# A graph network on one core: the state tables of layers 1 to 3 transposed in 32x32 blocks by VectorE and joined by four stores, with a feature's two parts side by side

## The chip, the cores and the metric

The kernel runs on one core of a Trainium2 chip. The metric is device time in microseconds (us), the median of several runs. A core has five engines, each with its own program, joined by semaphores: TensorE (PE, matmuls; its weight loads are PEld), VectorE (DVE), ScalarE (ACT), GpSimd (POOL) and SyncE (SP). Here SyncE issues nearly all plain DMAs, and GpSimd the gathers.

## What is computed

A graph network over 12500 nodes and 200000 edges (sorted by dst): a layernorm, an encoder, five rounds of message passing with a GRU update, a decoder. All of it is float32.

```python
h = relu(layernorm(x)); h = relu(h @ enc_w1.T + enc_b1) @ enc_w2.T + enc_b2
for w in conv_w:                                   # 5 layers
    agg = segment_sum((h @ w)[src], dst, n_nodes)
    gi = agg @ gru_wih.T + gru_bih
    gh = h @ gru_whh.T + gru_bhh
    r, z = sigmoid(gi_r + gh_r), sigmoid(gi_z + gh_z)
    n = tanh(gi_n + r * gh_n)
    h = (1 - z) * n + z * h
out = x + sigmoid(relu(relu(h) @ dec_w1.T + dec_b1) @ dec_w2.T + dec_b2)
```

## The kernel before

**States and tables.** The matrices of a layer are folded into the GRU's (W_FOLD), so that sums of old states are enough. States are held twice in DRAM: transposed (features on partitions) in `states`, one block of 128x512 for each of 25 chunks of 512 nodes (the last has 256), and with a node to a row in `table[0]` and `table[1]`, of which a layer reads one and writes the other. A row has 1 KB: 128 features, each as two float32 parts. The high part is the state rounded to fp32r, the form in which TensorE takes it, and the low part is what is left. Before, the 128 high parts stand first and the 128 low parts behind them.

**Two ways to a sum.** A chunk's sums come in one of two ways.
- *Strips*, for the first 14 chunks (11 in layer 0): TensorE multiplies the whole table, resident in SBUF as `parts` (98 blocks of 128 nodes), by a matrix of edge counts. Counts are loaded as bytes (SP, L705), three pieces of 448 KB in a ring, widened by ScalarE (L1126) and used in `sum_unit` (L1908): for each of 98 blocks two matmuls, one with the high and one with the low parts as weights, both with 512 count columns.
- *Gathers*, for the rest: GpSimd gathers 128 rows of the table at a time (L940), eight gathers to a group of edges, with room for four groups in `messages`. TensorE multiplies a group by a selection that VectorE makes (L1410, L1801), VectorE adds the high and the low half (`combine`, L1441), TensorE transposes (L1808) and VectorE adds it to `running` (L1459).

**Order of the work.** `Stage` cuts a layer into steps, one for each group (84 in layers 1 to 4). Every engine's program walks the same steps. `spread_gru` sets the step at which each chunk's GRU begins, at least three apart, and `gru_steps` then gives the chunk's stage t in each step: t = 1 gates (TensorE L1817 to L1824, ScalarE L1051), t = 2 the candidate's input, t = 3 VectorE's `after_candidate` (L1513, L1516, L1526), which ends in h_new, t = 4 the table, t = 5 its store. Strip pieces are spread over the steps, and the first of the next layer fill the end.

**The table, t = 4.** TensorE's `make_table` waits for h_new and transposes its four 128x128 blocks into PSUM (L1743); ScalarE copies them rounded into the high parts of `table_stage` (L1076); VectorE subtracts these from PSUM into the low parts (`low_halves`, L1322). At t = 5 SyncE stores a chunk at once (L626). The last chunk of a layer is chunk 24; its gates follow chunk 23's table in each program.

**Layer's end.** GpSimd's first gather of a layer waits for all 25 chunks' stores (L950). SyncE loads `parts` in seven portions (L711).

## Time and profile before

| | us |
|---|---|
| median of 3 runs | 4876.18 |
| lowest, highest | 4873.26, 4878.4 |
| the profiled execution | 4887.71 |
| its span | 4886.0 |

| engine | busy us | share of the span |
|---|---|---|
| TensorE | 4569.3 | 94% |
| its weight loads | 3509.0 | 72% |
| ScalarE | 3776.9 | 77% |
| GpSimd | 3514.1 | 72% |
| VectorE | 2125.1 | 43% |

Busy time leaves out the work of issuing and waiting. A gather's own time counts as GpSimd's, and what it moves as the DMA engines'. Times of the trace count from the start of the span. Gathers of the five layers run at 155 to 1278, 1313 to 2172, 2195 to 3054, 3076 to 3934 and 3957 to 4855 us. L12 is line 12 of the kernel before.

### The profile page before, as it was taken

Reading aid. Unit: us, or ns where it says so; the run is one execution under the profiler, and the core shown is the slowest. Engines: PE = TensorE matmul, PEld = TensorE weight load, DVE = VectorE, ACT = ScalarE, POOL = GpSimd, SP = SyncE. Lnnn points to the kernel's source line nnn. Section 1 sums busy time; section 2 is a strip of 40 time slices with the busy share of each in tenths; the row PEclk is TensorE's granted clock in tenths of the full one; section 3 lists DMA queues with packets and bytes.
Section 4 is the critical chain, followed back from the end, with each engine's and each line's share of the span. In section 5 each row is a group of like instructions: output and inputs, shape, how many; then the busy total and the mean of one; then the engine's idle time right before and its main releaser. Section 6 shows DMA issues by size and latency. Waiting matters only on the chain.

```text
span 4886.0 us, 65093 instructions
## 1 busy us (share of the span) xinstructions
PE 4569.3 (94%) x21620; PEld 3509.0 (72%) x21620; DVE 2125.1 (43%) x5051; ACT 3776.9 (77%) x3018; POOL 3514.1 (72%) x3618
## 2 busy tenths in 40 slices
PE   5579999998899999989999999899999989999998
PEld 3357767676677777767777777677777767777775
DVE  7678888787323333332333233233323323232324
ACT  5468889888688787858888786788888767787784
POOL 3577777777577777767777777677777767777675
PEclk8789999999999999999999999999999999999999
DMA  6899999999877777787777779777777877777774
GB/s 208 280 288 281 292 288 286 286 288 307 275 231 242 237 242 237 241 287 246 237 241 240 236 242 309 227 239 236 248 229 251 289 238 226 219 216 219 218 219 150
DMA packets 712057, 1217.93 MB, mean 249 GB/s; under 512 B 283649, under 2 KB 442370, under 8 KB 711618
## 3 DMA queue, kind: packets, MB, share of 16 engines
q1 hardware_dynamic: 538976, 741.62, 49.2%
q0 software_dynamic: 172336, 470.52, 30.7%
q8 instruction: 176, 2.88, 0.2%
q10 hardware_dynamic: 434, 1.81, 0.1%
q14 instruction: 135, 1.11, 0.1%
HBM read 1017.20 MB, written 196.41 MB: 248 GB/s over the span
## 4 chain that ended last, share of the span: by engine, by line
PE 71%; ACT 7%; POOL 6%; DMA 6%; issue 5%; DVE 4%; SPq 0%; DVEq 0%; ACTq 0%; POOLq 0%
PE strip_ps L1908 34%; PE four_ps L1908 16%; POOL messages L940 6%; ACT counts L1126 4%; PE agg_ps L1801 4%; DMA raw<-adjacency 3%; PE four_ps L1801 3%; ACT room L1101 2%; PE r_ps L1817 2%; PE z_ps L1817 2%; PE r_ps L1823 2%; PE z_ps L1823 2%; PE four_ps L1824 1%; PE r_ps L1830 1%; PE four_ps L1894 1%
## 5 line engine op out<-in xcount | busy, mean ns | idle before, releaser
L940 POOL DMA_INDIRECT messages<-table,src_stage x3567 | 3467.0, 972 | 1278.6 <-issue 1121.6
L1126 ACT ACTIVATE counts<-raw 128x2048 fp32r<-128x2048 uint8 x1354 | 2227.5, 1692 | 429.0 <-PE strip_ps L1908 239.9
L1908 PE MATMUL strip_ps<-counts,parts 128*128 128x512 f32 x9016 | 2283.0, 406 | 62.3 <-ACT counts L1126 49.5
L1908 PEld LDWEIGHTS strip_ps<-counts,parts 128*128 128x128 f32 x9016 | 1690.2, 190 | 508.5 <-issue 117.5
L1908 PE MATMUL four_ps<-counts,parts 128*128 128x512 f32 x4116 | 985.4, 396 | 0.0
L1126 ACT ACTIVATE counts<-third_raw 128x2048 fp32r<-128x2048 uint8 (+1 forms) x522 | 855.9, 1688 | 158.2 <-PE strip_ps L1908 87.9
L1908 PEld LDWEIGHTS four_ps<-counts,parts 128*128 128x128 f32 x4116 | 768.7, 188 | 184.0 <-issue 28.8
L1410 DVE TENSOR_TENSOR selection<-agg_ps,dst_stage 128x1024 fp32r<-128x1024 bf16 x277 | 337.3, 1218 | 947.4 <-PE agg_ps L1808 946.6
L1410 DVE TENSOR_TENSOR selection<-four_ps,dst_stage 128x1024 fp32r<-128x1024 bf16 (+1 forms) x172 | 207.8, 1208 | 860.2 <-PE four_ps L1808 860.0
L1101 ACT ACTIVATE room<-four_ps 128x784 uint16<-128x784 f32 x448 | 359.5, 822 | 89.9 <-PE four_ps L1894 47.1
L1801 PE MATMUL agg_ps<-messages,selection 128*128 128x256 f32 x2211 | 339.9, 297 | 40.2 <-DMA messages<-table,src_stage 39.1
L1801 PEld LDWEIGHTS agg_ps<-messages,selection 128*128 128x128 f32 x2211 | 291.7, 195 | 64.1 <-DMA messages<-table,src_stage 43.6
L1801 PE MATMUL four_ps<-messages,selection 128*128 128x256 f32 x1356 | 205.2, 294 | 19.9 <-DMA messages<-table,src_stage 19.9
L1801 PEld LDWEIGHTS four_ps<-messages,selection 128*128 128x128 f32 x1356 | 173.7, 190 | 38.1 <-DMA messages<-table,src_stage 22.9
L1070 ACT ACTIVATE gate_n<-gate_r,b 128x512 f32<-128x512 f32 (+1 forms) x125 | 88.5, 708 | 104.4 <-DVE gate_r L1493 96.8
L1441 DVE TENSOR_REDUCE rows<-agg_ps 128x128 f32<-128x256 f32 x277 | 116.0, 419 | 117.0 <-PE agg_ps L1801 116.7
L1051 ACT ACTIVATE gate_r<-r_ps,b_rz 128x512 f32<-128x512 f32 (+1 forms) x100 | 67.4, 674 | 101.7 <-PE r_ps L1823 101.7
L1322 DVE TENSOR_TENSOR table_stage<-four_ps,table_stage 128x512 fp32r<-128x512 f32 (+1 forms) x75 | 51.1, 681 | 202.9 <-ACT table_stage L1076 202.4
L1441 DVE TENSOR_REDUCE rows<-four_ps 128x128 f32<-128x256 f32 x172 | 69.5, 404 | 141.5 <-PE four_ps L1801 141.5
L1817 PE MATMUL r_ps<-h_old,w 128*128 128x512 f32 (+1 forms) x200 | 105.3, 609 | 6.0 <-DMA h_old<-states 5.9
L1817 PE MATMUL z_ps<-h_old,w 128*128 128x512 f32 (+1 forms) x200 | 104.9, 608 | 0.0
L1824 PE MATMUL four_ps<-h_old,w 128*128 128x512 f32 (+1 forms) x200 | 100.7, 585 | 0.0
(226 smaller groups left out, 3575.3 us busy)
## 6 DMA issues: line engine op xcount, KB each, us to landing
raw<-adjacency SPq DMA_DIRECT2D x677, 448.0 KB, 5.2
third_raw<-adjacency SPq DMA_DIRECT2D x261, 448.0 KB
adjacency<-room SPq DMA_DIRECT2D x112, 784.0 KB
parts<-table SPq DMA_DIRECT2D x35, 1792.0 KB, 14.2
messages<-table,src_stage POOLq DMA_INDIRECT x3567
table<-table_stage SPq DMA_DIRECT2D x108, 512.0 KB, 3.0
h_old<-states SPq DMA_DIRECT2D x120, 256.0 KB
states<-h_new SPq DMA_DIRECT2D x108, 256.0 KB, 3.2
```

What stands on the lines that cost most here:

```text
L940: nc.gpsimd.indirect_dma_start(messages[:, slot, t, :, :].rearrange("p i f -> p (i f)").bitcast(F32), None, table[k.layer % 2], bass.Indir ...
L1051: nc.scalar.activation(gate_r[:, 0:n], r_ps[:, 0:n], ACT.Sigmoid, bias=b_rz[:, R:R + 1]).then_inc(gates_rz, 1)
L1070: nc.scalar.activation(gate_n[:, 0:n], pre_n[:, 0:n], ACT.Tanh, bias=b[:, B_IH + N:B_IH + N + 1]).then_inc(cand, 1)
L1101: nc.scalar.activation(eighth_counts[:, eighth % 2, :, j * SET_NODES // 2:(j + 1) * SET_NODES // 2].rearrange("p k (t d) -> p k t d", t=SE ...
L1126: nc.scalar.activation(to, raw_piece[:, :, a * EIGHTH:e * EIGHTH].rearrange("p q (k d) -> p k q d", d=EIGHTH), ACT.Copy).then_inc(expanded, 1)
L1410: ops.tensor_tensor(selection[:, s % 2, 0:n, :], on_each(cols_ps[k.agg_bank(s)].bitcast(BF16), n), along(dst_stage[:, at:at + n], ROWS), A ...
L1441: ops.tensor_reduce(rows[:, :], agg_ps[k.agg_bank(s)][:, 0:2 * H].rearrange("p (i f) -> p f i", i=2), AX_X, ALU.add).then_inc(combined, 1)
L1801: last = mm(agg_ps[k.agg_bank(s)][:, 0:2 * H], selection[:, s % 2, t, :], messages[:, slot, t, :, :].rearrange("p i f -> p (i f)"), start= ...
L1817: mm(bank[:, 0:n], wblock(W_HH + gate), h[:, 0:n], start=True, stop=False)
L1823: mm(bank[:, 0:n], wblock(W_FOLD + gate), a[:, 0:n], start=False, stop=True).then_inc(gates_ps, 1)
L1824: mm(hn_ps[:, 0:n], wblock(W_HH + N), h[:, 0:n], start=True, stop=True).then_inc(gates_ps, 1)
L1908: last = mm(strip_banks[k.bank_of(i)], parts[:, block, half, :], counts[:, 0 if k.first else p % 2, at, :], start=(p == 0 and at == 0 and ...
```

## The change

In layers 1 to 3 TensorE no longer makes the table. After h_new VectorE transposes it in 32x32 blocks (`turn_state`) into `turned`, which is the buffer of `diff`. Partition 32q + r then holds, in columns 32m to 32m + 31, the features 32q to 32q + 31 of node 32m + r. ScalarE copies `turned` rounded into the high parts, VectorE subtracts in place of `low_halves`, and SyncE puts a chunk's rows together with four stores, one for each block of 32 partitions, in runs of 64 words (256 B). So that a run holds both parts, the table's rows now have a feature's high and low part side by side, everywhere: `parts`, the first table, layer 0, and the addition in `combine`. Stores are counted by `tables_stored(n)`. Layer 0 still transposes on TensorE, the last layer makes no table. The path `general` (other graphs) isn't run.

```diff
+def tables_stored(n):
+    return 16 * (n + (QUARTERS - 1) * max(0, n - 2 * CHUNKS))
...
-        by_half = table_stage[:, :].bitcast(F32R).rearrange("p (j i f) -> p j i f", i=2, f=H)
+        by_half = table_stage[:, :].bitcast(F32R).rearrange("p (j f i) -> p j i f", i=2, f=H)
+        by_quarter = table_stage[:, :].bitcast(F32R).rearrange("p (n f i) -> p n i f", i=2, f=QUARTER)
...
-        relu_h, decT = gate_n, diff
+        relu_h, decT, turned = gate_n, diff, diff
...
-        parts = sb("parts", [P, BLOCKS, 2, H], F32R)
+        parts = sb("parts", [P, BLOCKS, H, 2], F32R)
...
+            def store_turned_table(t, u, c, j):
+
+                sp.wait_ge(table_out, u + 1)
+                to = table[t][c * CHUNK:c * CHUNK + j * P, :].rearrange("(n r) (q e) -> r q n e", r=QUARTER, q=QUARTERS)
+                for q in range(QUARTERS):
+                    sp.dma_start(to[:, q, :, :], table_stage[q * QUARTER:(q + 1) * QUARTER, 0:j * 2 * H].rearrange("r (n e) -> r n e", e=2 * QUARTER)).then_inc(table_stored, 16)
...
-                pool.wait_ge(table_stored, 16 * CHUNKS * (k.layer + 1))
+                pool.wait_ge(table_stored, tables_stored(CHUNKS * (k.layer + 1)))
...
+            def make_turned_table(v, j):
+
+                act.wait_ge(table_sum, v + (CHUNKS + 1))
+                act.wait_ge(table_stored, tables_stored(v + CHUNKS))
+                nc.scalar.activation(by_quarter[:, 0:j * QUARTERS, 0, :], turned[:, 0:j * P].rearrange("p (q f) -> p q f", f=QUARTER), ACT.Copy).then_inc(table_hi, 1)
...
+            def turn_state(v, j):
+
+                dve.wait_ge(gru, 5 * v + 5)
+                ops.transpose(turned[:, 0:j * P], h_new[:, 0:j * P]).then_inc(table_sum, 1)
+
+            def turned_low_halves(u, j):
+
+                dve.wait_ge(table_hi, u + 1)
+                ops.tensor_tensor(by_quarter[:, 0:j * QUARTERS, 1, :], turned[:, 0:j * P].rearrange("p (q f) -> p q f", f=QUARTER),
+                                  by_quarter[:, 0:j * QUARTERS, 0, :], ALU.subtract).then_inc(table_out, 1)
...
-                ops.tensor_reduce(rows[:, :], agg_ps[k.agg_bank(s)][:, 0:2 * H].rearrange("p (i f) -> p f i", i=2), AX_X, ALU.add).then_inc(combined, 1)
+                ops.tensor_reduce(rows[:, :], agg_ps[k.agg_bank(s)][:, 0:2 * H].rearrange("p (f i) -> p f i", i=2), AX_X, ALU.add).then_inc(combined, 1)
...
                 if t == 3:
                     after_candidate(layer, v, n, j, h)
+                    if not last_layer:
+                        turn_state(v, j)
                 if t == 4 and not last_layer:
-                    low_halves(v + CHUNKS, j)
+                    turned_low_halves(v + CHUNKS, j)
...
-                        last = mm(strip_banks[k.bank_of(i)], parts[:, block, half, :], counts[:, 0 if k.first else p % 2, at, :],
+                        last = mm(strip_banks[k.bank_of(i)], parts[:, block, :, half], counts[:, 0 if k.first else p % 2, at, :],
...
-                if t == 4:
-                    (decode_first(n, J) if last_layer else make_table(k.layer, v, J))
+                if t == 4 and last_layer:
+                    decode_first(n, J)
```

How this moves instructions, at three places. TensorE at the end of layer 3, before: the last groups of edges, chunk 23's transposes, then the last chunk's gates (`running` is its sums) and its two transposes.

```order
L1801 MATMUL four_ps<-messages,selection 128x256 x3
L1808 MATMUL four_ps<-identity,rows 128x128
L1743 MATMUL four_ps<-identity,h_new 128x128 x4
L1817 MATMUL r_ps<-h_old,w 128x256
L1817 MATMUL z_ps<-h_old,w 128x256
L1823 MATMUL r_ps<-running,w 128x256
L1823 MATMUL z_ps<-running,w 128x256
L1824 MATMUL four_ps<-h_old,w 128x256
L1830 MATMUL r_ps<-running,w 128x256
L1743 MATMUL four_ps<-identity,h_new 128x128 x2
L1908 MATMUL strip_ps<-counts,parts 128x512 x112
```

And now (line numbers are those of the changed kernel):

```order
L1838 MATMUL four_ps<-messages,selection 128x256 x3
L1845 MATMUL four_ps<-identity,rows 128x128
L1854 MATMUL r_ps<-h_old,w 128x256
L1854 MATMUL z_ps<-h_old,w 128x256
L1860 MATMUL r_ps<-running,w 128x256
L1860 MATMUL z_ps<-running,w 128x256
L1861 MATMUL four_ps<-h_old,w 128x256
L1867 MATMUL r_ps<-running,w 128x256
L1945 MATMUL strip_ps<-counts,parts 128x512 x112
```

Nothing in TensorE's program stands between the last sums and the last gates any more. VectorE in layer 2, before, from a chunk's h_new to its table (`selection` is of the next group of edges, `rows` its combined sums):

```order
L1526 TENSOR_TENSOR h_new<-diff,gate_n 128x512
L1410 TENSOR_TENSOR selection<-agg_ps,dst_stage 128x1024
L1453 TENSOR_LOAD starts
L1453 ISA x2
L1459 ISA
L1459 TENSOR_TENSOR running<-running,agg_ps 128x128
L1441 TENSOR_REDUCE rows<-four_ps 128x128
L1322 TENSOR_TENSOR table_stage<-four_ps,table_stage 128x4x128
```

And now, for the same chunk:

```order
L1561 TENSOR_TENSOR h_new<-diff,gate_n 128x512
L1351 STREAM_TRANSPOSE diff<-h_new 128x512
L1445 TENSOR_TENSOR selection<-agg_ps,dst_stage 128x1024
L1488 TENSOR_LOAD starts
L1488 ISA x2
L1494 ISA
L1494 TENSOR_TENSOR running<-running,agg_ps 128x128
L1476 TENSOR_REDUCE rows<-four_ps 128x128
L1356 TENSOR_TENSOR table_stage<-diff,table_stage 128x512
```

The block transposes stand between h_new and the next group's selection, and the subtraction reads `diff` in SBUF rather than a PSUM bank. SyncE in layer 1, around a store, before:

```order
L620 DMA states<-h_new 128x512
L668 DMA h_old<-states 128x512
L705 DMA raw<-adjacency 128x3584 x2
L705 DMA third_raw<-adjacency 128x3584
L626 DMA table<-table_stage 128x4x256
L705 DMA raw<-adjacency 128x3584 x2
```

And now:

```order
L629 DMA states<-h_new 128x512
L684 DMA h_old<-states 128x512
L723 DMA raw<-adjacency 128x3584 x2
L723 DMA third_raw<-adjacency 128x3584
L642 DMA table<-table_stage 32x16x64 x4
L723 DMA raw<-adjacency 128x3584 x2
```

One store of 512 rows of 256 words is now four of 512 runs of 64 words.

## Rows read from the trace of the kernel before

**Rows 1.** The page: span, and busy time, share of the span and instructions by engine.

```profile
span 4886.0 us, 65093 instructions
...
PE 4569.3 (94%) x21620; PEld 3509.0 (72%) x21620; DVE 2125.1 (43%) x5051; ACT 3776.9 (77%) x3018; POOL 3514.1 (72%) x3618
```

**Rows 2.** Busy time by stage: after layer 1, layer 2, layer 4; columns as headed.

```profile
core 0: us, PE busy (x) PEld busy (x) DVE busy (x) ACT busy (x) POOL busy (x), PEclk, DMA share, GB/s
...
2171.90:2194.80 22.90, 11.89 (x32) 7.82 (x32) 11.01 (x23) 6.76 (x9) 0.01 (x1) 0.57 0.40 134
2194.80:3053.90 859.10, 852.58 (x3876) 667.61 (x3876) 263.60 (x467) 684.23 (x484) 652.09 (x675) 0.99 0.80 250
...
3956.60:4855.40 898.80, 873.97 (x3933) 674.90 (x3933) 275.91 (x484) 695.14 (x519) 652.29 (x675) 0.99 0.71 218
```

**Rows 3.** GpSimd's waits in layer 2 (first row) and layer 4: us, times, longest.

```profile
POOL messages L940 <- PE four_ps L1801: 0.9, 3, 0.3
...
POOL messages L940 <- PE agg_ps L1801: 31.3, 16, 4.3
```

**Rows 4.** The gathers of layer 2: duration in ns, min/median/max.

```profile
L940 POOL DMA_INDIRECT messages<-table,src_stage x675: 949/956/1469, 2194.8 to 3052.9; - x169
```

**Rows 5.** GpSimd in order of time, layer 2: start us, duration us.

```profile
2325.03 0.95 POOL L940 DMA_INDIRECT messages<-table,src_stage  x1 [0.30 <-issue]
2326.28 1.40 POOL L940 DMA_INDIRECT messages<-table,src_stage  x1 [0.30 <-issue]
2327.99 1.15 POOL L940 DMA_INDIRECT messages<-table,src_stage  x1 [0.30 <-issue]
```

**Rows 6.** VectorE at the same time.

```profile
2324.50 1.22 DVE L1410 TENSOR_TENSOR selection<-four_ps,dst_stage 128x1024 fp32r<-128x1024 bf16 x1 [3.69 <-PE four_ps L1808]
...
2326.17 0.68 DVE L1513 TENSOR_TENSOR diff<-h_old,gate_n 128x512 f32<-128x512 f32 x1
...
2327.61 0.69 DVE L1526 TENSOR_TENSOR h_new<-diff,gate_n 128x512 f32<-128x512 f32 x1
```

**Rows 7.** Groups by shape: the table's transposes, copy and subtraction.

```profile
L1743 PE MATMUL four_ps<-identity,h_new 128*128 128x128 f32 x344 | 55.1, 284 | 24.2 <-DVE h_new L1526 15.7 <-DVE room L1317 8.5
L1322 DVE TENSOR_TENSOR table_stage<-four_ps,table_stage 128x512 fp32r<-128x512 f32 x72 | 49.8, 691 | 199.6 <-ACT table_stage L1076 199.1
...
L1076 ACT ACTIVATE table_stage<-four_ps 128x512 fp32r<-128x512 f32 x72 | 41.7, 579 | 45.4 <-PE four_ps L1743 44.7 <-DMA table<-table_stage 0.7
```

**Rows 8.** TensorE in layer 2: a group's weight loads, and strip matmuls.

```profile
2604.87 1.02 PEld L1801 LDWEIGHTS four_ps<-messages,selection 128*128 128x128 f32 x8
...
2610.26 6.96 PE L1908 MATMUL four_ps<-counts,parts 128*128 128x512 f32 x28
```

**Rows 9.** The SP queue in 494:496 and in 2184.5:2187.5: packets, MB, share.

```profile
q1 hardware_dynamic: 880, 0.39, 68.2%
...
q1 hardware_dynamic: 528, 0.52, 50.8%
```

**Rows 10.** All engines at the end of layer 1, in order of time.

```profile
2179.53 0.29 DVE L1459 TENSOR_TENSOR running<-running,four_ps 128x128 f32 x1 [0.78 <-PE four_ps L1808]
...
2181.18 0.69 DVE L1526 TENSOR_TENSOR h_new<-diff,gate_n 128x512 f32<-128x512 f32 x1
...
2181.93 1.11 PE L1743 MATMUL four_ps<-identity,h_new 128*128 128x128 f32 x4 [2.65 <-DVE h_new L1526]
...
2182.84 1.06 PE L1817 MATMUL r_ps<-h_old,w 128*128 128x256 f32 x2
...
2186.25 0.84 PE L1824 MATMUL four_ps<-h_old,w 128*128 128x256 f32 x2
...
2189.62 0.42 DVE L1526 TENSOR_TENSOR h_new<-diff,gate_n 128x256 f32<-128x256 f32 x1
...
2191.68 0.37 SPq L626 DMA_DIRECT2D table<-table_stage  x1
...
2194.79 0.95 POOL L940 DMA_INDIRECT messages<-table,src_stage  x1 [22.90 <-DMA table<-table_stage]
```

More of the change, by code:

```diff
@@ L46 @@
 PLACE = 2 * H
+QUARTER = 32
+QUARTERS = P // QUARTER
 STEPS = CHUNK // GROUP_NODES
@@ L468, in by_sub @@
             return values.rearrange("p (k e) -> p k e", e=P)
-        first_halves = [stage.bitcast(F32R).rearrange("p (j i f) -> p j i f", i=2, f=H) for stage in first_stages]
+        first_halves = [stage.bitcast(F32R).rearrange("p (j f i) -> p j i f", i=2, f=H) for stage in first_stages]
         edges_of = edges.rearrange("p (k i e) -> p k i e", i=2, e=P)
@@ L674, in new_state, with new_table @@
                     load_x(n, c, j)
-            def new_table(layer, v, n, c, j):
-                if layer < LAYERS - 1:
+            def new_table(layer, v, n, c, j, turned_here=False):
+                if layer == LAYERS - 1:
+                    store_out(n, c, j)
+                elif turned_here:
+                    store_turned_table((layer + 1) % 2, v + CHUNKS, c, j)
+                else:
                     store_table((layer + 1) % 2, v + CHUNKS, c, j)
-                else:
-                    store_out(n, c, j)
             def store_eighth(e):
@@ L707, in load_portion @@
             def load_portion(layer, portion, stored):
-                sp.wait_ge(table_stored, 16 * (CHUNKS * layer + stored + 1))
+                sp.wait_ge(table_stored, tables_stored(CHUNKS * layer + stored + 1))
                 a = portion * PORTION
-                sp.dma_start(parts[:, a:a + PORTION, :, :].rearrange("p k i f -> p k (i f)").bitcast(F32),
+                sp.dma_start(parts[:, a:a + PORTION, :, :].rearrange("p k f i -> p k (f i)").bitcast(F32),
                              table[layer % 2][a * P:(a + PORTION) * P, :].rearrange("(k p) f -> p k f", p=P)).then_inc(parts_loaded[portion], 16)
@@ L831, in states_and_tables @@
                         if t == (7 if last_layer else 5):
-                            new_table(layer, v, n, chunk, j)
+                            new_table(layer, v, n, chunk, j, True)
                 if layer == 1:
@@ L1671, in one_tile @@
                     dve.wait_ge(g_gathered[layer], 16 * (t + 1))
-                    ops.tensor_tensor(tile_messages, tile_halves[:, 0:H], tile_halves[:, H:2 * H], ALU.add).then_inc(g_step[layer], 1)
+                    ops.tensor_tensor(tile_messages, tile_by_part[:, :, 0], tile_by_part[:, :, 1], ALU.add).then_inc(g_step[layer], 1)
                     dve.wait_ge(g_step[layer], g + 4)
@@ L2016, in last_chunk_step @@
                         gate_n_input(v, LAST_J, running)
-                    if t == 4:
-                        (decode_first(n, LAST_J) if last_layer else make_table(layer, v, LAST_J))
+                    if t == 4 and last_layer:
+                        decode_first(n, LAST_J)
                     if t == 5 and last_layer:
```

9 lines of the change are left out of this document (5 added, 4 removed).

## The prediction

> **What bounds the kernel now.** I read the busy shares first. TensorE is busy for 94% of the span [rows 1], which suggests that whatever frees it frees time. The table by stage shows more. In layer 2, from its first gather to the end of its last, 675 gathers go out in 859.1 us, or 1.273 us each, and TensorE is busy for 852.6 us of it [rows 2]: both engines are full. Who waits for whom decides between them. In layer 2 GpSimd waits for TensorE for less than 2 us in all; in layer 4 it waits 31 us for one bank of TensorE's alone [rows 3]. The median gather keeps GpSimd busy for 0.956 us [rows 4], and 0.30 us later the next one follows [rows 5], so 675 undisturbed gathers take 675 x 1.26 = 850 us. Layer 2 takes 9 us more than that. So in layers 1 to 3, whose tables the change touches, **GpSimd's chain of gathers sets the pace**, and TensorE only keeps up, with up to four groups of room between them. A TensorE instruction removed there buys nothing by itself. What counts is what lengthens a gather, and the 22.9 us in which GpSimd stands idle between layers, when TensorE is busy for half of the time, at a mean granted clock of 0.57, so mostly at the lower of its two levels, 1.2 GHz [rows 2].
>
> **What lengthens a gather.** At 2325.03 one takes 0.95 us, the next two 1.40 and 1.15 us [rows 5]. VectorE was then in the three operations that make h_new, each with two operands in SBUF [rows 6]. The gather at 2325.03 ran under the selection, whose other operand is in PSUM, and was not stretched. Over layer 2 the gathers' busy time is 652.1 us [rows 2] against 675 x 0.956 = 645.3: 6.8 us over 25 chunks, 0.27 us a chunk, about **0.09 us for each operation with two SBUF operands**. The Trainium skill (Advanced Engine Details and Errata, GPSIMD Details) names the reason: GpSimd shares a read and a write interface with VectorE, in conflict when VectorE has two SBUF inputs. It speaks against this change, and the trace agrees, with 1.40 us beside 0.95. By that rule alone the block transposes below, with one input, would cost GpSimd nothing unless they run in a two-port mode, and the sum would be 2 us lower.
>
> **The change, part by part.**
>
> *Low halves.* They were hi subtracted from PSUM (0.69 us, one PSUM operand [rows 7]). Both operands are now in SBUF. Length: the same as L1526's, 0.69 us [rows 6], hidden on VectorE, which is busy for 31% of layer 2 [rows 2]. Its cost is on GpSimd: 25 x 0.09 = 2.3 us a layer, **+6.8 us for three layers**. Bounds: 0, if it always falls between the gathers' sensitive moments, and 0.2 us a chunk (15 us), from the 0.45 that the worst gather in rows 5 gained.
>
> *Block transposes.* One 128x512 on VectorE a chunk. No row shows this operation. By the nearest ones, 512 elements from SBUF [rows 6], it takes about 0.69 us. It has a single SBUF operand, as the selection has, which shows no harm, but it stands right behind the three that do. GpSimd: 0 to 0.09 us each; I take a third: **+2 us** for 75, range 0 to 7. Queued behind it on VectorE is the selection for the next group, 0.7 us later; TensorE reads that a whole step later.
>
> *TensorE.* It loses 294 transposes (four for each of 24 chunks and two for the last, three times), at most 55.1/344 = 0.16 us each [rows 7], 47 us in all. I cost this at **nothing**: the cover is the chain of gathers, which goes on at 1.26 us. If that cover went, by a faster gather, up to 16 us a layer would be had.
>
> *ScalarE's copy* reads SBUF rather than PSUM and writes every other word: 0.58 us now [rows 7]; nothing on the path inside a layer. Should the strided write double it, that is 25 x 0.6 = 15 us a layer, against 175 us that ScalarE is idle in layer 2 [rows 2]: still nothing. The interleaved write is new in the first table and in layer 0 too, with the same answer.
>
> *The weight load of the strips* now takes every second word of parts. Twenty-eight strip matmuls take 6.96 us, at most 0.249 each, while the eight loads of a group come in 1.02 us, at most 0.128 each [rows 8]. So a load could take nearly twice as long and hide under its matmul. I cost it at 0. The skill (SBUF — State Buffer, Door 1) has 16-byte lines that give full bandwidth from two hits on; two 4-byte words at a step of 8 are exactly two. No row here shows such a read.
>
> *Stores.* One store of 512 packets of 1 KB becomes four of 512 packets of 256 B. A lone store in the quiet end of layer 1 held the queue 50.8% of 3 us on 16 engines: 24.4/528 = 46 ns a packet [rows 9]. In the crowd of layer 0, mostly 448 B packets took 68.2% of 2 us x 16 over 880, 25 ns [rows 9]. So 2048 x 25 ns / 16 = 3.2 us in place of 1.5, or 25 x 1.7 = 43 us a layer: the DMA share of layer 2 goes from 0.80 to 0.85 [rows 2]. Bounds: 1.8 us if bytes alone counted (25 x 256/448 = 14 ns), and 5.9 us if a small packet cost the 46 ns of 1 KB. SyncE issues three more, 0.38 us each [rows 10]; its next work is a raw piece, and three are in the ring. Inside a layer: nothing. The skill (DMA: Bandwidth & Descriptors, Specifications) wants 512 B or more and has a read-modify-write below; 25 ns for 448 B shows no such price, and by the rule the share would be higher, still without a wait on the gathers.
>
> *The end of a layer* is the second place where time is made. Now TensorE, in program order, waits for h_new of chunk 23 (2181.87), transposes it and only then begins the gates of the last chunk at 2182.84, though that chunk's sums were there at 2179.82 [rows 10]. With the transposes gone, the five gate products start at about 2179.4 and end near 2183.7 rather than 2187.1. What is late next is ScalarE: it takes chunk 23's table copy before the last gates, and that copy waits for h_new and the block transposes, 2182.6, so reset and update gates end at 2184.2. From the last gate product to h_new took 2.95 us (2187.09 to 2190.04); the same steps from 2184.2 give the last h_new at about 2187.2. From there to the store's issue it was 1.64 us [rows 10], some 0.9 of it copy and subtraction. But the copy must wait until chunk 23's four stores have landed. They go out from 2184.0, and with 3.2 us to move and about 1 us around it they land at about 2188.3. So the last chunk's stores go out at 2189.2 rather than 2191.68, and four of them (1.5 us to issue, 1024 packets) land about 1.2 us later after that than the one did. Gain 2.5 - 1.2 = 1.3; I take **-1.2 us, three times: -3.6**. Bounds: -2.5 if the stores cost nothing more, +1.5 if a 256 B packet costs as much as one of 1 KB.
>
> **Sum.** 6.8 + 2 - 3.6 = +5.2 us. The profiled execution took 4887.7 us (span 4886.0), so it would take 4892.9. The runs' median is 4876.2, 11.5 lower; on that basis **4881.5 us**. A measurement of this kernel can tell about 0.2%, 9.8 us: the forecast is no change.
>
> **Rivals.**
> - *GpSimd is hurt more.* The transposes hold the shared interface as the two-operand operations do, and a lone operation costs more than a third of a block of three (0.45 us for one gather [rows 5]). At 0.2 to 0.3 us a chunk: +15 to +22 less 3.6, **4888 to 4896**. For: gathers are back to back, no operation can miss them all. Against: the mean of 0.27 us for three. Chance of more than +9.8 us: 0.2.
> - *The weight loads don't hide.* From a load of 0.25 us on, TensorE is the bound. At 0.264, say, each strip matmul costs 15 ns more: 14 strips x 98 blocks x 2 parts = 2744 of them are 41 us a layer, of which 16 are paid by the transposes gone and 7 by the present slack, leaving some 18 in layers 1 to 3 and 41 in layer 4 and 32 in layer 0: **about 5000**. Chance 0.08, with DMA crowding that delays raw pieces.
> - *The layer's end gives more and GpSimd loses nothing.* -2.5 x 3 and 0: **4869**; a little more and it is measurably faster. For: TensorE's 2.65 us wait for h_new goes entirely. Chance of over 9.8 us: 0.12.
>
> That leaves 0.60 for the forecast. The range leaves out the weight loads and both outer corners: 4868 (no harm, full gain) to 4898 (0.3 us a chunk, and the last stores as slow as 1 KB packets). Faster 0.12, same 0.60, slower 0.28.
>
> **What would show it.** Right: layers 1 to 3 take 861 to 863 us from first to last gather, their gathers busy for 655 us rather than 652; GpSimd's idle time after layers 1, 2 and 3 falls from 22.9 to about 21.7 us and not after layer 0; TensorE's busy time in layer 2 falls by 11 to 16 us and it waits for messages instead; 28 strip matmuls still take 6.96 us; layer 4 stays at 899 us. Wrong: strip matmuls further apart, layer 4 longer, GpSimd waiting for TensorE in layer 2, or a gather undisturbed under the new subtraction.

## The result and the profile after

The changed kernel took **4900.28 us** (median of 5 runs, 4890.82 to 4904.98), the kernel before 4876.18 us (median of 5, 4871.38 to 4878.4). The ratio is 1.0047, with a 95% interval of 1.0036 to 1.0059: slower by about 23 us. The forecast was 4881.5, no change, with a range up to 4898. It was wrong, on the slow side.

The page of the changed kernel. Beside [rows 1], TensorE has 294 instructions fewer and is busy for 20 us longer.

```profile
span 4898.5 us, 64730 instructions
...
PE 4589.8 (94%) x21326; PEld 3540.5 (72%) x21326; DVE 2177.5 (44%) x5126; ACT 3800.0 (78%) x3018; POOL 3523.4 (72%) x3618
...
DMA packets 828553, 1217.92 MB, mean 249 GB/s; under 512 B 437777, under 2 KB 558866, under 8 KB 828114
```

Busy time by stage of the changed kernel (the stretch after layer 1, layer 2, layer 4), which answers [rows 2]:

```profile
core 0: us, PE busy (x) PEld busy (x) DVE busy (x) ACT busy (x) POOL busy (x), PEclk, DMA share, GB/s
...
2166.90:2189.60 22.70, 11.25 (x29) 7.64 (x29) 12.68 (x25) 7.63 (x9) 0.00 (x0) 0.65 0.53 153
2189.60:3052.20 862.60, 854.00 (x3781) 670.21 (x3780) 278.68 (x487) 689.67 (x484) 655.09 (x675) 1.00 0.81 249
3961.20:4866.70 905.50, 884.13 (x3925) 686.75 (x3924) 275.45 (x483) 695.15 (x518) 653.06 (x675) 0.99 0.71 216
```

Four things stand here. Layer 2 takes 862.6 us, 3.5 more, and its gathers are busy for 655.1 us, 3.0 more: as forecast. The stretch after layer 1 is 22.7 us, where 21.7 was forecast. And **layer 4, whose own code the change touches only in how it reads its weights and sums its halves, takes 905.5 us, 6.7 more, with TensorE busy for 10 us more**. TensorE in layer 2 lost 95 records and gained 1.4 us.

That TensorE sets the pace of layer 4 is seen in GpSimd's waits for it there (us, times, longest). In the kernel before they are 31.3 us for one bank [rows 3] and, for the other,

```profile
POOL messages L940 <- PE four_ps L1801: 16.8, 14, 2.4
```

and in the changed kernel

```profile
POOL messages L958 <- PE agg_ps L1838: 33.5, 18, 4.1
...
POOL messages L958 <- PE four_ps L1838: 23.0, 19, 2.8
```

So 48.1 us of waiting became 56.5, 8.4 more, in a layer that is 6.7 us longer.

What TensorE does longer is seen in its weight loads. Layer 2's strips, the kernel before first, then the changed one; duration in ns, min/median/max:

```profile
L1908 PEld LDWEIGHTS four_ps<-counts,parts x1372: 187/188/192, 2233.5 to 3017.5; 128*128 128x128 f32 x196
```

```profile
L1945 PEld LDWEIGHTS four_ps<-counts,parts x1372: 192/193/198, 2228.4 to 3016.5; 128*128 128x128 f32 x196
```

Twenty-eight strip matmuls in a row went from the 6.96 us of [rows 8] to 7.09 (TensorE of the changed kernel in order of time):

```profile
2607.03 7.09 PE L1945 MATMUL four_ps<-counts,parts 128*128 128x512 f32 x28
```

From start to start, averaged over some 2700 strip matmuls of a layer, that is 227.7 ns before and 233.1 ns after. The load takes 188 and 193. The rest, 40 ns, is the same.

The end of layer 1 in the changed kernel, all engines in order of time. It answers [rows 10].

```profile
2174.75 1.06 PE L1854 MATMUL r_ps<-h_old,w 128*128 128x256 f32 x2
...
2176.86 0.69 DVE L1561 TENSOR_TENSOR h_new<-diff,gate_n 128x512 f32<-128x512 f32 x1
...
2177.59 0.71 DVE L1351 STREAM_TRANSPOSE diff<-h_new 128x512 f32<-128x512 f32 x1
...
2179.75 2.22 SPq L642 DMA_DIRECT2D table<-table_stage  x4
...
2182.11 0.42 DVE L1561 TENSOR_TENSOR h_new<-diff,gate_n 128x256 f32<-128x256 f32 x1
...
2184.57 0.43 ACT L1100 ACTIVATE table_stage<-diff 128x256 fp32r<-128x256 f32 x1 [3.41 <-DMA table<-table_stage]
...
2185.48 1.82 SPq L642 DMA_DIRECT2D table<-table_stage  x4
```

The last gates start before chunk 23's new state is there, and the last new state is ready 15.6 us after the last gather's end, 2.5 us earlier than before: as forecast. Then its copy waits until 2184.57 for chunk 23's four stores, and four more stores go out one after the other. GpSimd goes on at 2189.62, 4.14 us after the first of them was issued, where it was 3.11 after the one of before [rows 10].

### The profile page after: what moved, and what is told of

Same layout as the page of the kernel before. It is cut to its first block, busy times and chain, and to the rows that moved or that the text cites. A ratio compares the mean times of both kernels' runs of the same rounds, so it can differ in the third digit from the quotient of the medians.

```text
span 4898.5 us, 64730 instructions
## 1 busy us (share of the span) xinstructions
PE 4589.8 (94%) x21326; PEld 3540.5 (72%) x21326; DVE 2177.5 (44%) x5126; ACT 3800.0 (78%) x3018; POOL 3523.4 (72%) x3618
## 4 chain that ended last, share of the span: by engine, by line
PE 63%; POOL 14%; issue 7%; DMA 6%; ACT 6%; DVE 3%; SPq 0%; DVEq 0%; POOLq 0%; ACTq 0%
PE strip_ps L1945 31%; PE four_ps L1945 15%; POOL messages L958 14%; ACT counts L1150 4%; PE agg_ps L1838 3%; DMA raw<-adjacency 3%; PE four_ps L1838 3%; PE r_ps L1854 1%; PE z_ps L1854 1%; ACT room L1125 1%; PE r_ps L1860 1%; PE z_ps L1860 1%; PE four_ps L1861 1%; PE r_ps L1867 1%; DMA adjacency<-room 1%
## 5 line engine op out<-in xcount | busy, mean ns | idle before, releaser
L1945 PE MATMUL strip_ps<-counts,parts 128*128 128x512 f32 x9016 | 2314.9, 409 | 73.9 <-ACT counts L1150 61.3
L1945 PEld LDWEIGHTS strip_ps<-counts,parts 128*128 128x128 f32 x9016 | 1735.3, 195 | 507.4 <-issue 125.9
L1945 PE MATMUL four_ps<-counts,parts 128*128 128x512 f32 x4116 | 1005.2, 400 | 0.0
L1945 PEld LDWEIGHTS four_ps<-counts,parts 128*128 128x128 f32 x4116 | 790.8, 193 | 183.0 <-issue 28.1
L1356 DVE TENSOR_TENSOR table_stage<-diff,table_stage 128x512 fp32r<-128x512 f32 (+1 forms) x75 | 51.3, 684 | 197.5 <-ACT table_stage L1100 197.5
```

The source lines that it names most:

```text
L1945: last = mm(strip_banks[k.bank_of(i)], parts[:, block, :, half], counts[:, 0 if k.first else p % 2, at, :], start=(p == 0 and at == 0 and ...
```

## How the kernels below are compared

The stretch after layer 0 took between 22 and 34 us in the profiles with no pattern by edit (34.2 before, 26.8 in the changed kernel, 23.8 in e1, 32.9 in e10b and e8c). So a span says less than the ratio over all runs, and the profiles are read by stage. The profiled execution of the kernel before is also 11.5 us above the median of its runs, so that its span and the changed kernel's are 12.5 us apart where the medians are 24. The intervals of the ratios reach some 0.1% to either side; worked out from two such intervals, an estimate is that two edited kernels must lie 0.15%, or 7 us, apart before their ratios alone tell which is faster. Worked out from the gathers of each profile, from the start of a layer's first to the end of its last, and the idle time of GpSimd between:

```
                            layers 1, 2, 3        idle after 1, 2, 3  layer 4  idle after 3   strip matmul
                                                                               plus layer 4   to the next
before                      859.3  859.1  858.1   22.9  22.0  22.5    898.9    921.4          227.7 ns
changed                     862.7  862.6  861.6   22.7  23.0  24.4    905.6    929.9          233.1
e1  weights in a row        863.3  862.2  860.9   21.2  22.2  23.6    896.0    919.7          227.6
e2  layout only             862.9  865.5  865.6   20.3  21.1  21.2    911.5    932.7          233.1
e3  one store               862.2  863.8  862.6   20.1  18.8  19.2    907.9    927.2          233.1
e4  short runs              860.7  860.3  861.1   25.4  25.1  25.6    892.2    917.8          227.6
e10b e1 and e3              861.0  862.0  861.7   19.9  19.3  19.8    900.0    919.7          227.7
e8c own stage               861.3  861.8  860.8   21.9  17.5  22.7    902.9    925.6          233.1
e7c before, gates first     858.2  857.1  857.1   19.9  19.8  20.0    896.8    916.8          227.7
e9b e7 and own stage        857.7  857.1  856.3   20.8  20.6  20.6    898.4    919.0          227.7
```

The last two columns go together: with weights at every second word the idle time before layer 4 and layer 4 make 926 to 933 us, with weights in a row 917 to 921, however the idle time itself comes out. A reading that fits is that TensorE runs ahead while GpSimd idles, and layer 4 gives the head start back; no run tests it alone.

Each line is one execution. Layers 1 to 3 are 1 to 2 us shorter each in e7 and e9, whose edits touch only the ends of layers, than in the profile of the kernel before. A difference of that size in one layer says little by itself.

## The experiments

Theory A: the strided weights make each strip matmul dearer by 5.5 ns, which lengthens layer 4 and eats what the transposes free. Rivals: layer 4 is longer for another reason (B), or the slower weights lengthen layers 1 to 3 too (C). The four stores are the second suspect, the gathers' stretch the third.

**Weights in a row (e1).**

```diff
-  mm(strip_banks[...], parts[:, block, :, half], counts...)
+  mm(strip_banks[...], parts[:, block, :, :].rearrange("p f i -> p (f i)")[:, half * H:(half + 1) * H], counts...)
```

> The changed kernel with one edit: each strip matmul reads its weights as 128 words in a row again instead of every second word, so a strip sums a mixture of both parts of half the features (the part left wrong is the strips' sums; the work is the same in number and shape). Theory A (every second word makes each strip matmul 5 to 6 ns dearer): the distance of strip matmuls goes back from 233 to 227 ns, layer 4 from 905.5 to about 899 us, TensorE's busy time in layer 2 falls below 852; layers 1 to 3 keep their 862.6 us, since GpSimd sets their pace. Time 4900 - 7 = 4893. Rival B (layer 4 is longer through the longer rows' interleaving on VectorE or through the transfers): layer 4 stays at 905 and the time at 4900. Rival C (the slower weights also lengthen layers 1 to 3): these fall to 859 to 860 each, time 4883 to 4886.

Measured: 4884.64 us, ratio to the kernel before 1.0019 (1.0009 to 1.0028). The strips' sums are then not the right ones, the work is the same. That gives back 0.28%, 14 us (give or take 7), of the 0.47%. The distance is 227.6 ns again, layer 4 took 896.0 us, and layers 1 to 3 stayed. Its layer 2, and its strips on the page:

```profile
2187.80:3050.10 862.30, 844.24 (x3781) 658.39 (x3780) 279.36 (x487) 684.68 (x484) 654.60 (x675) 0.99 0.81 249
```

```profile
L1945 PE MATMUL strip_ps<-counts,parts 128*128 128x512 f32 x9016 | 2279.0, 406 | 76.5 <-ACT counts L1150 63.6
L1945 PEld LDWEIGHTS strip_ps<-counts,parts 128*128 128x128 f32 x9016 | 1689.4, 190 | 520.2 <-issue 128.9
```

GpSimd's waits for TensorE in its layer 4 are 47.3 us in all, about what they were before the change:

```profile
POOL messages L958 <- PE agg_ps L1838: 30.7, 16, 7.3
...
POOL messages L958 <- PE four_ps L1838: 16.6, 14, 2.4
```

TensorE is busy for 844.2 us in a layer 2 of the same length as with 854.0: there its 10 us are idle time and no more, in layer 4 they are time. A holds, B and C don't. The gain by the ratios is twice the 7 us expected, though their noise leaves room for 7: in the profiles layer 4 gave 9.5 of it, and the idle times after layers 1 to 3 were 3 us shorter in sum, which nothing here explains.

**The layout alone, on the kernel before (e2).** Tables still turned by TensorE, stored whole.

```diff
-  by_half = table_stage[:, :]...rearrange("p (j i f) -> p j i f", i=2, f=H)
+  by_half = table_stage[:, :]...rearrange("p (j f i) -> p j i f", i=2, f=H)
-  parts = sb("parts", [P, BLOCKS, 2, H], F32R)
+  parts = sb("parts", [P, BLOCKS, H, 2], F32R)
-  mm(strip_banks[...], parts[:, block, half, :], counts...)
+  mm(strip_banks[...], parts[:, block, :, half], counts...)
```

> The kernel before with the new row layout alone (a feature's two parts side by side, strips' weights at every second word); tables still turned by TensorE and stored whole. Theory A: distance of strip matmuls 233 ns, layer 4 905 us; without the transposes' relief TensorE needs 852.6 + 2744 x 0.0055 = 868 us in each of layers 1 to 3, above GpSimd's 859, so these become 866 to 869 us; time 4876 + 6.7 + 3 x 8 = about 4907, 4900 to 4912. Rival B (the layout costs nothing, the strips are slower for another reason): 4876, 227 ns, layer 4 at 899.

Measured: 4904.86 us, ratio 1.0066 (1.0050 to 1.0083). A again. Layer 2 now has a bound that it had neither before nor after, and GpSimd waits for TensorE in it (its waits in layer 2: us, times, longest):

```profile
2188.70:3054.30 865.60, 862.66 (x3863) 680.86 (x3863) 262.57 (x463) 689.26 (x483) 650.62 (x675) 1.00 0.79 247
```

```profile
POOL messages L941 <- PE agg_ps L1802: 9.5, 11, 2.7
POOL messages L941 <- PE four_ps L1802: 4.5, 9, 1.3
```

TensorE is busy for all but 3 us of 865.6, while the gathers, not stretched here (busy for 650.6 us), would have allowed the 859 us of the kernel before. So TensorE's freed transposes did buy something: they paid for the slower strips in layers 1 to 3. In layer 4, which makes no table, nothing paid. Layer 4 took 911.5 us here, 6 more than in the changed kernel with the same distance of 233.1 ns; those 6 are not explained.

**One store a chunk (e3).**

```diff
-  for q in range(QUARTERS):
-      sp.dma_start(to[:, q, :, :], table_stage[q * QUARTER:(q + 1) * QUARTER, 0:j * 2 * H]...)
+  sp.dma_start(chunk_rows(table[t], c, j), by_tile(table_stage, j, 2 * H))
```

> The changed kernel with one store per chunk of 1 KB runs, as before, in place of the four of 256 B (rows of the tables land in the wrong places: that is the part left wrong). If four small-packet stores make the layers' ends as slow as they are: GpSimd's idle time after layers 1, 2 and 3 falls from 22.7 to 24.3 us to about 21 to 21.5, layers themselves stay at 862 us, time 4900 - 6 = 4894. Rival (the stores' packets also crowd the gathers inside a layer): layers 1 to 3 fall by 1 us or more each as well, time 4888 to 4891. Rival (the end is set by copy and subtraction, not by stores): idle time unchanged, 4900.

Measured: 4891.06 us, ratio 1.0036 (1.0024 to 1.0049), 0.11% or 5 us better than the changed kernel, which the ratios alone can't tell from nothing. The rows of the tables land in the wrong places, the work is the same but for the stores. The layers did not get shorter: packets crowd nothing inside a layer. The idle times after layers 1, 2 and 3 fell by 2.7, 4.2 and 5.1 us, of which about half of the last is given back in layer 4 (927.2 beside 929.9 us). The end of its layer 1:

```profile
2184.14 0.42 DVE L1559 TENSOR_TENSOR h_new<-diff,gate_n 128x256 f32<-128x256 f32 x1
...
2185.08 0.43 ACT L1098 ACTIVATE table_stage<-diff 128x256 fp32r<-128x256 f32 x1 [1.89 <-DVE diff L1349]
...
2186.00 0.37 SPq L640 DMA_DIRECT2D table<-table_stage  x1
...
2189.09 0.95 POOL L956 DMA_INDIRECT messages<-table,src_stage  x1 [20.05 <-DMA table<-table_stage]
```

From the last new state to the copy 0.5 us, where the changed kernel has 2.0; from the store's issue to the next gather 3.09 us, where it has 4.14. The four stores cost 1.5 us of waiting and 1.05 us of issue and landing, 2.6 us at this layer's end, about what the earlier gates had brought there (2.5). After layers 2 and 3 the idle time fell by more than these 2.6 us, which is not explained.

**Weights in a row and 128 B runs (e4).** The row layout of before (first parts, then second parts), so that the sums are right with weights in a row; the turned table goes out by eight stores a chunk.

```diff
-  parts = sb("parts", [P, BLOCKS, H, 2], F32R)
+  parts = sb("parts", [P, BLOCKS, 2, H], F32R)
-  to = ...rearrange("(n r) (q e) -> r q n e", r=QUARTER, q=QUARTERS)
+  to = ...rearrange("(n r) (i q e) -> r i q n e", r=QUARTER, i=2, q=QUARTERS)
   for q in range(QUARTERS):
-      sp.dma_start(to[:, q, :, :], ...)
+      for i in range(2):
+          sp.dma_start(to[:, i, q, :, :], by_quarter[q * QUARTER:(q + 1) * QUARTER, 0:j * QUARTERS, i, :]...)
```

> The changed kernel with the row layout of before (first parts in a row, then second parts), so that weights are read in a row, and the turned table stored by eight stores a chunk with 128 B runs. Theory A: distance of strip matmuls 227 ns, layer 4 899 us, time 4900 - 7 from there. Eight stores of 128 B: 4096 packets a chunk; inside a layer hidden, at its end 1 to 3 us more idle than with four: +3 to +9. Together 4896 to 4902. If small packets crowd the gathers' transfers, layers 1 to 3 grow beyond 863 us: 4905 or more.

Measured: 4889.67 us, ratio 1.0031 (1.0020 to 1.0043). Better than the changed kernel by 0.16%, 8 us, at the edge of the noise, and below what was expected. Twice as many stores lengthen the idle times to 25.1 to 25.6 us, nothing inside the layers; the weights in a row are worth more.

**Both costs away (e10).** e1 and e3 together.

> The changed kernel with both suspected costs taken away: the strips' weights read in a row and one store of 1 KB runs a chunk (sums and places of rows are left wrong). If slower weights (16 us) and the four stores (9 us) make the difference to the kernel before, with the longer gathers (10 us) set against TensorE's earlier last gates: 4900 - 16 - 9 = 4875, a ratio of 1.000 to the kernel before, layers 1 to 3 at 862 us, idle times after them 19 to 20 us, layer 4 at 896 to 900. Rival (the two overlap, one standing in the other's shadow): the gain is no more than the larger, 4884, ratio 1.002.

> Both suspected costs taken away from the changed kernel once more, since the last chip took 5929 us for the kernel before as well. If they add up: 4900 - 16 - 9 = 4875, ratio 1.000 to the kernel before, layers 1 to 3 at 862 us, idle times after them 19 to 20 us, layer 4 at 896 to 900. Rival (one stands in the other's shadow): 4884, ratio 1.002.

The first run fell on a chip where everything takes a fifth longer (below): 5912.36 beside 5929.43, ratio 0.9955 (0.9921 to 0.9990). The second: 4881.21 us, ratio 1.0008 (0.9997 to 1.0018). So 0.39% came back, and 0.28 and 0.11 were the parts: **they add up**, as far as parts with a noise of 0.15% each can show it. The rival's 1.002 lies just above the interval. From e3 to this run, on the same chip, the weights alone are worth 0.28% once more. In microseconds 0.39% is 19 rather than the 25 expected, which had been summed from single medians (16 and 9) and not from ratios. What is left is 4 us by the ratio, with an interval that holds zero, and 7 by the medians. In the profiles layers 1 to 3 are 8.2 us longer in sum than in the kernel before and the idle times after them 8.4 shorter: the gathers' stretch against the earlier last gates.

**One more subtraction, one more transposition on the kernel before (e5, e6).**

```diff
   low_halves(v + CHUNKS, j)
+  ops.tensor_tensor(diff[:, 0:j * P], h_new[:, 0:j * P], gate_n[:, 0:j * P], ALU.subtract)
```

```diff
   after_candidate(layer, v, n, j, h)
+  if not last_layer:
+      dve.wait_ge(gru, 5 * v + 5)
+      ops.transpose(diff[:, 0:j * P], h_new[:, 0:j * P])
```

> The kernel before with one more VectorE operation per chunk in layers 1 to 3: a subtraction of two SBUF tiles of 512 columns, right behind the low halves, whose result nothing reads. If two SBUF operands stretch the gathers beside them (by 0.09 us an operation, as the prediction had it): GpSimd's busy time in each of layers 1 to 3 grows by 2.3 us, from 652 to about 654.3, the layers from 859 to 861.3; time 4873 + 7 = 4880. If a lone operation costs more than a third of the block of three: up to 3.4 us a layer, 4883. Rival (the stretch in the changed kernel comes from elsewhere): 652 and 859, 4873.

> The kernel before with one more VectorE operation per chunk in layers 1 to 3: the 32x32 block transposition of the new state, at the place where the changed kernel has it, whose result nothing reads. As the prediction had it (one SBUF operand, a third of a two-operand operation): +0.7 us a layer, GpSimd busy 652.8; time 4875. Rival (a transposition holds the shared way as the two-operand operations do): +1.5 to 3 us a layer, GpSimd busy 653.5 to 655, time 4878 to 4882. With the extra subtraction's number the two should add up to the 3.4 us a layer that the changed kernel is longer, if its gathers are stretched by these two operations and nothing else.

> The extra subtraction once more, since the chip of its first run took 5858 us for the kernel before as well. If two SBUF operands stretch the gathers beside them: GpSimd's busy time in each of layers 1 to 3 grows from 652 to about 654.3, the layers from 859 to 861.3; time 4873 + 7 = 4880; up to 3.4 us a layer and 4883 if a lone operation costs more than a third of the block of three. Rival (the stretch comes from elsewhere): 652 and 859, 4873.

> The extra block transposition once more. As the prediction had it: +0.7 us a layer, GpSimd busy 652.8; time 4875. Rival (a transposition holds the shared way as two-operand operations do): +1.5 to 3 us a layer, GpSimd busy 653.5 to 655, time 4878 to 4882.

All four runs fell on a chip on which the kernel before takes 5857 us. The ratios were 0.9998, 0.9990, 0.9989 and 1.0014, each with an interval of 0.003 to 0.004 to either side, which tells nothing of 7 us. The gathers' busy time can still be compared, with e7 on the same chip in the place of the kernel before. Layer 2 of e7, e5 and e6 in their second runs:

```profile
2700.00:3732.00 1032.00, 912.47 (x3829) 684.91 (x3827) 259.71 (x451) 683.06 (x480) 650.70 (x675) 0.93 0.66 206
```

```profile
2669.70:3699.60 1029.90, 916.89 (x3857) 689.60 (x3857) 274.37 (x479) 685.18 (x481) 653.23 (x675) 0.94 0.67 207
```

```profile
2660.00:3674.60 1014.60, 909.12 (x3844) 685.92 (x3844) 275.14 (x476) 684.05 (x481) 652.80 (x675) 0.94 0.68 210
```

Over layers 1 to 3 of both runs the mean is 652.0 us for e7 (650.8 to 653.5), 653.7 with the subtraction (653.3 to 655.0) and 652.2 with the transposition (651.9 to 652.8). The two edited kernels differ by 1.5 us a layer, 0.06 us for each operation: the subtraction, with two operands in SBUF, stretches the gathers more than the transposition, with one. The Trainium skill (Advanced Engine Details and Errata, GPSIMD Details) has a conflict on the shared interface when VectorE has two SBUF inputs: the 1.5 us between the two agree with that.

What each costs by itself is less sure, since it hangs on e7. By e7 the subtraction costs 1.7 us a layer and the transposition 0.3, together 2.0 of the 3.3 by which the gathers of the changed kernel are longer. But in its profile at 4866 us e7 has 650.3 us a layer where the kernel before has 651.8, a difference as large. In the profiles of the table above, four kernels without VectorE's new work (before, e2, e7c, e9b) have 649.9 to 651.8 us a layer and six with it (changed, e1, e3, e4, e8c, e10b) 653.6 to 655.6. So the stretch comes with the turned tables; its split into subtraction, transposition and a rest of 1.3 is not shown. Writing every other word is not enough for it, since e2 does so too (650.6). ScalarE's copy, which now reads SBUF, was not tried alone.

**A stage of its own for the last chunk's table (e8).** On the changed kernel.

```diff
-  act.wait_ge(table_stored, tables_stored(v + CHUNKS))
-  nc.scalar.activation(by_quarter[:, ...
+  act.wait_ge(table_stored, tables_stored(v + CHUNKS - (j == LAST_J)))
+  nc.scalar.activation(quarters_of(j)[:, ...
-  sp.dma_start(to[:, q, :, :], table_stage[...
+  sp.dma_start(to[:, q, :, :], (strip_sum if j == LAST_J else table_stage)[...
...
+  if i == 0 and layer > 1:
+      dve.wait_ge(table_stored, tables_stored(CHUNKS * (layer + 1)))
```

The stage is `strip_sum`, which the strips use too; so VectorE's first copy into it in the next layer waits for all stores.

> The changed kernel with one edit: the last chunk's table of layers 1 to 3 is staged in a buffer of its own, so that its copy doesn't wait until chunk 23's four stores have landed. If that wait holds the layer's end: GpSimd's idle time after layers 1, 2, 3 falls by 1 to 2 us each from 22.7, 23.0, 24.4; time 4900 - 4 = 4896. Rival (the last stores land late because they stand behind chunk 23's on the same queue, whatever the staging): the copy is earlier, the idle time the same, 4900.

> The changed kernel with a stage of its own for the last chunk's table, once more. If the wait for chunk 23's four stores holds the layer's end: GpSimd's idle time after layers 1, 2, 3 falls by 1 to 2 us each from 22.7, 23.0, 24.4; time 4900 - 4 = 4896. Rival (the last stores stand behind chunk 23's on the same queue, whatever the staging): idle time the same, 4900.

> The changed kernel with a stage of its own for the last chunk's table, on a chip on which the kernel before takes 4874 us if it comes out so. If the wait for chunk 23's four stores holds the layer's end: idle times of GpSimd after layers 1, 2, 3 fall by 1 to 2 us each from 22.7, 23.0, 24.4; time 4896. Rival: idle times the same, 4900.

On the slow chip 5849.72 and 5836.01 us, ratios 0.9988 (0.9956 to 1.0020) and 0.9983 (0.9946 to 1.0021): undecided. On another chip, where the kernel before takes 4873.72 us, it took 4889.22, ratio 1.0034 (1.0021 to 1.0047), 0.13% or 6 us better than the changed kernel, which the ratios alone can't tell from nothing; 4 was expected. The end of its layer 1:

```profile
2185.30 0.43 DVE L1566 TENSOR_TENSOR h_new<-diff,gate_n 128x256 f32<-128x256 f32 x1
...
2186.23 0.43 ACT L1105 ACTIVATE strip_sum<-diff 128x256 fp32r<-128x256 f32 x1 [1.89 <-DMA table<-table_stage]
...
2187.15 1.82 SPq L647 DMA_DIRECT2D table<-strip_sum  x4
...
2191.31 0.95 POOL L963 DMA_INDIRECT messages<-table,src_stage  x1 [21.94 <-DMA table<-strip_sum]
```

The copy follows the new state after 0.5 us, and the 1.5 us of waiting are gone; from the first store to the next gather it is 4.16 us still. So the two halves of the stores' cost are apart: waiting for the stage, and issuing and landing four. The idle times fell by 0.8, 5.5 and 1.7 us, where 1 to 2 each were expected. After layer 1 the last new state itself came 0.7 us later here (16.3 us after the last gather, 15.6 in the changed kernel); the 5.5 are not explained.

**The last chunk's gates first, on the kernel before (e7).** The only gain that the change brought, without the change.

```diff
-  for chunk, t in k.active(step):
+  for chunk, t in sorted(k.active(step), key=lambda at: step == k.steps and at[0] != LAST):
...
-  active = k.active(step)
+  active = sorted(k.active(step), key=lambda at: step == k.steps and at[0] != LAST)
```

> The kernel before with one edit: in the step after the last group TensorE and ScalarE take the gates of the last chunk before the table of chunk 23. If the layer's end hangs on TensorE waiting for chunk 23's new state ahead of the last gates: idle time of GpSimd after layers 1 and 2 falls from 22.9 and 22.0 us by 1.5 to 2.5 each, after layer 3 too, but layer 4, whose pace is TensorE's, gives that back; time 4873 - 4 = 4869, 4867 to 4871. Rival (the stores' landing, not the gates, sets it): no change, 4873.

> The kernel before with the last chunk's gates ahead of chunk 23's table, once more. If the layer's end hangs on TensorE waiting for chunk 23's new state: idle time of GpSimd after layers 1 and 2 falls from 22.9 and 22.0 us by 1.5 to 2.5 each; time 4873 - 4 = 4869. Rival (the stores' landing sets it): no change, 4873.

> The kernel before with the last chunk's gates first, without the own stage: both together gave 12.6 us. If the gates' order gives most of it, since TensorE then never waits for chunk 23's state: ratio 0.9980, about 4865, idle times after layers 1 and 2 down by 1.5 to 2.5 us. If the own stage gave most of it: ratio 0.9992 or above, 4870 to 4874.

On the slow chip 5836.9 and 5841.51 us, ratios 0.9982 (0.9949 to 1.0015) and 0.9967 (0.9926 to 1.0008). On the other chip **4864.00 us, ratio 0.9974 (0.9963 to 0.9984)**. The end of its layer 1:

```profile
2180.00 0.43 DVE L1526 TENSOR_TENSOR h_new<-diff,gate_n 128x256 f32<-128x256 f32 x1
...
2181.82 0.37 SPq L626 DMA_DIRECT2D table<-table_stage  x1
...
2184.91 0.95 POOL L940 DMA_INDIRECT messages<-table,src_stage  x1 [19.86 <-DMA table<-table_stage]
```

The idle times are 3.0, 2.2 and 2.5 us shorter. The medians are 9.7 us apart, and the profiles show 11 us at the places that the edit touches: 5.2 after layers 1 and 2, 4.6 in the idle time after layer 3 and layer 4 together, and 1.6 behind the last gather. They are 21 us apart as a whole: of the other 10, 6 lie in layer 0 and the stretch after it and 4 in layers 1 to 3, neither of which the edit touches.

**Both on the kernel before (e9).** e7 with the last chunk's table in a stage of its own.

> The kernel before with two edits at the layers' ends: the last chunk's gates ahead of chunk 23's table on TensorE and ScalarE, and a stage of its own for the last chunk's table in layers 1 to 3. If TensorE's wait for chunk 23's state and the wait for chunk 23's store each hold the end: GpSimd's idle time after layers 1 and 2 falls by 2 to 3 us each from 22.9 and 22.0; layers keep 859 us, and what is gained ahead of layer 4 is given back in it, since TensorE sets its pace. Time 0.9988 to 0.9992 of the kernel before (4873 to about 4868). Rival (the store's landing alone sets the end): ratio 1.0.

> The kernel before with both edits at the layers' ends, once more. If each holds the end: GpSimd's idle time after layers 1 and 2 falls by 2 to 3 us each from 22.9 and 22.0, ratio 0.9988 to 0.9992. Rival (the store's landing alone sets the end): ratio 1.0, idle times the same.

First on a slow chip (5905.36 beside 5929.43, ratio 0.9969, 0.9943 to 0.9995), then 4861.39 us, **ratio 0.9971 (0.9958 to 0.9984)**. The same as e7 within the intervals: with one store, issued and landed early, e7's last copy has no stage to wait for (it starts 0.5 us after the last new state), so a second stage has nothing to save. Either version beats both kernels.

## Why the prediction was wrong, point by point

- **The weight loads, costed at 0: the step that failed.** It read "a load could take nearly twice as long and hide under its matmul", and took the load's length from rows of the message weights [rows 8]. The strips' own loads take 188 ns, and the distance of two strip matmuls is load plus 40 ns at either length: nothing of the added 5 ns hides, they cost 5.4 to 5.5 ns every time. That is 15 us of TensorE's time a layer. In layers 1 to 3 the removed transposes paid it (e2 shows the bill without them: 865.6 us), in layer 4 nothing did. By the table, the idle time before layer 4 and layer 4 took 8.5 us more, by e1's ratio all of it 14 us, give or take 7. The prediction had named two signs of this, strip matmuls further apart and a longer layer 4, and both came. The rival "the weight loads don't hide" had the mechanism, a price of 15 ns and a threshold at a load of 0.25 us. The price was too high, and the cost began far below that threshold, between 188 and 193 ns. The Trainium skill (SBUF — State Buffer, Door 1) was cited for full bandwidth at a step of two words; the trace has 193 beside 188 ns, so it is not quite full.
- **The end of a layer, -3.6 us: came out +2.6.** The sums with their size were right up to the last new state (2.5 us earlier), and the landing of four stores cost 1.05 us, where 1.2 stood. The term that was mis-sized is the wait for chunk 23's stores. The stores of the last chunk were to go out 2.5 us earlier; they went out 1.2 us earlier (18.6 us after the last gather, 19.8 before). Chunk 23's state came 0.7 us later than before, and its four stores needed 4.8 us from the first issue until the copy could start, where the text had 4.3.
- **The gathers, +8.8 us: right.** 3.4, 3.5 and 3.5 us a layer, 10.4 in sum. That the turned tables bring it is shown; its split isn't. The subtraction costs 1.5 us a layer more than the transposition, where 2.3 less 0.7 was forecast.
- **TensorE's transposes, costed at nothing: right in layers 1 to 3,** since e1 took 10 us off TensorE there and nothing changed. "Busy time falls by 11 to 16 us" was wrong, mostly by the weights: it rose by 1.4. With weights in a row (e1) it fell by 8.3, still less than 11.
- **Stores inside a layer, nothing: right** (e3): with one store a chunk the layers got no shorter. The DMA share of layer 2 is 0.81, where 0.85 was forecast.
- **The sum.** Off by 19 us: some 7 to 14 from the weights (7 is layer 4 alone), 6 from the ends of the layers and 2 from the gathers. The range ended at 4898 because, in its own words, it left the weight loads out. In the first rival 22 less 3.6 gives 4895, not 4896, which changes nothing.

## What to carry to other kernels

When an edit changes how an operand is read, measure the distance between instructions of that very kind against their parts before calling anything hidden. The strips' own load of 188 ns and their distance of 227.7 were in the trace of before, beside the 128 ns that the prediction used; that a longer load would not hide took a second length of load to see. Multiply even 3% by the number of instructions, in every stage that reads the operand, and above all in the one where the engine is the bound and nothing was removed. If a change brings two things, ask whether the useful one (here the order of the last gates) can be had alone.

## What the runs showed of the hardware

- Reading fp32 weights at every second word makes the 128x128 load 193 rather than 188 ns, in all of some 2700 a layer, and each matmul with 512 columns follows the last after load plus 40 ns (227.7 and 233.1). At the lower clock the loads took 330 and 331 ns and the median distance was 427 ns with either reading, so the cost showed at the higher clock alone.
- A 32x32 block transposition of 128x512 fp32 takes VectorE 0.71 us, of 128x256 0.45 us.
- Four stores in a row are issued 0.5 us apart: 1.82 us for four, where one takes 0.37.
- Chips differ. The edited kernels' runs above of 4861 to 4905 us are from two chips; on two others the kernel before took 5857 and 5929 us. The edited kernels moved the same bytes there at 206 to 209 GB/s rather than 249, at a mean granted clock of 0.91 to 0.92 rather than 0.97. ScalarE's widening of the counts (L1126) waited 682 us in e7's second run for what the profile puts outside this core, and has no such wait in the profile of the kernel before. The differences told apart here are lost in the scatter there, all but two: e9 and e10 stood below the kernel before (0.9969 and 0.9955, intervals short of 1). For e10 this is not what it gave on the faster chip (1.0008, 0.9997 to 1.0018), so a ratio does not carry over from one chip to the other.
